# Seven of sixteen state sums moved from VectorE to ScalarE and GpSimd in a two-layer decoder kernel

## What is computed

```python
x = ln(x + mamba(x))            # E=512 channels, N=16 states; stages "pre", "skip", "scan", "out"
x = ln(x + context_softmax(x))  # kv = ctx @ Wk; softmax(norm(x @ kv kv^T))     stage "xat0"
x = ln(x + moe_ffn0(x))         # 8 experts of 176, top 2, shared 352           stage "ffn0"
x = ln(x + hgrn(x))             # gated linear scan over positions              stage "hgrn"
x = ln(x + adjacency(ctx))      # q k^T, top 76 of 256 in each row, sigmoid     stage "adj"
x = ln(x + moe_ffn1(x))         # 8 experts of 128, top 2, shared 256           stage "ffn1"
# mamba: for each state n of 16, over the positions l
state[n] = exp(dts * A[n]) * state[n] + dts * B[n] * hidden
y       += C[n] * state[n]      # then (y + D * hidden) * silu(gate) @ W_out
```

## Time and profile before

| | |
|---|---|
| time, median of 3 runs | 560.07 us (559.85 to 563.25) |
| the profiled execution | 561.63 us, its span 559.8 us |
| granted TensorE clock, mean | 0.938 of full speed |
| PE / PEld busy | 497.2 us (89%) / 435.6 us (78%) |
| DVE / ACT / POOL busy | 472.0 us (84%) / 365.0 us (65%) / 318.8 us (57%) |

### The profile page before, as it was taken

How to read it: one execution, slowest core, us unless ns; L and a number is a source line. 1 busy time by engine, 2 the same in 40 slices (tenths; PEclk the granted TensorE clock), 3 DMA queues, 4 the chain that set the end, 5 groups by cost and what they waited for, 6 DMA issues and landing times.

```text
span 559.8 us, 10385 instructions
## 1 busy us (share of the span) xinstructions
PE 497.2 (89%) x3304; PEld 435.6 (78%) x3304; DVE 472.0 (84%) x1053; ACT 365.0 (65%) x877; POOL 318.8 (57%) x465
## 2 busy tenths in 40 slices
PE   4857376868876999999999999999999999999996
PEld 3535264637765988888898998998999999999985
DVE  1399999979999899999999999999889997745451
ACT  2489967578957866689958797974976481350210
POOL 1056669853688677548946676795649443334042
PEclk9798568679996999999999999999999999999999
DMA  7612920003472454021530566436055206553000
GB/s 192 213 63 74 380 76 2 0 0 104 134 260 90 133 177 134 30 76 58 164 120 5 155 190 220 132 89 194 2 161 170 87 15 211 175 164 105 11 11 9
DMA packets 26517, 64.16 MB, mean 115 GB/s; under 512 B 4512, under 2 KB 8352, under 8 KB 26080
## 3 DMA queue, kind: packets, MB, share of 16 engines
q1 hardware_dynamic: 26464, 63.50, 35.9%
HBM read 62.38 MB, written 1.11 MB: 113 GB/s over the span
## 4 chain that ended last, share of the span: by engine, by line
PE 64%; DVE 16%; issue 8%; POOL 5%; ACT 4%; DMA 2%; SPq 0%; DVEq 0%; POOLq 0%; ACTq 0%
PE work L616 40%; PE work L670 13%; PE h_bank L592 6%; DVE acc L1197 5%; POOL dbu L545 4%; DVE st L1181 3%; PE work L592 2%; DVE m L1144 1%; PE h_bank L693 1%; ACT dA L964 1%; DVE wk L1148 1%; DMA b_rows<-b_dram 1%; DVE du L1113 1%; DVE bst L1016 1%; PE work L749 1%
## 5 line engine op out<-in xcount | busy, mean ns | idle before, releaser
L545 POOL TENSOR_TENSOR dbu<-du,b_rows 128x512 f32<-128x512 f32 x128 | 163.4, 1278 | 30.5 <-DVE du L1133 21.0
L964 ACT ACTIVATE dA<-dts,a_neg 128x127 f32<-128x127 f32 x512 | 156.6, 355 | 21.1 <-DVE st L1181 20.0
L1181 DVE TENSOR_TENSOR_SCAN st<-dA,dbu 128x512 f32<-128x512 f32 x128 | 155.1, 1214 | 3.3 <-ACT dA L964 2.7
L592 PE MATMUL h_bank<-ident,st 128*128 128x128 f32 x512 | 85.8, 302 | 32.8 <-DVE acc L1197 21.8
L616 PE MATMUL work<-xsT,stream 128*128 128x128 f32 x896 | 110.0, 278 | 0.8 <-DVE du L1113 0.7
L616 PEld LDWEIGHTS work<-xsT,stream 128*128 128x128 f32 x896 | 105.9, 194 | 2.8 <-DVE du L1113 0.9
L592 PEld LDWEIGHTS h_bank<-ident,st 128*128 128x128 f32 x512 | 66.3, 156 | 47.9 <-DVE st L1181 38.9
L1197 DVE SCALAR_TENSOR_TENSOR acc<-h_bank,c_cols,acc 128x512 f32<-128x512 f32 x128 | 93.2, 728 | 7.4 <-issue 3.4
L567 POOL TENSOR_TENSOR hb<-hb,wbt 128x512 f32<-128x512 f32 (+2 forms) x48 | 55.2, 1153 | 54.0 <-ACT wbt L836 36.3
L491 POOL TENSOR_SCALAR var<-mv 128x1 f32<-128x1 f32 x56 | 13.1, 234 | 83.5 <-DVE mv L1017 83.1
L670 PE MATMUL work<-stream,hb 128*128 128x256 f32 x224 | 53.6, 381 | 0.0
(11 more groups left out here) (157 smaller groups left out, 795.0 us busy)
## 6 DMA issues: line engine op xcount, KB each, us to landing
stream<-in_stream SPq DMA_DIRECT2D x48, 512.0 KB, 3.8
stream<-in_stream SPq DMA_DIRECT2D x48, 384.0 KB, 3.8
b_rows<-b_dram SPq DMA_DIRECT2D x32, 256.0 KB, 4.5
wg<-in_wg SPq DMA_DIRECT2D x1, 1280.0 KB, 7.7
wu<-in_wu SPq DMA_DIRECT2D x1, 1280.0 KB, 10.3
wd<-in_wd SPq DMA_DIRECT2D x1, 1280.0 KB, 12.9
xT<-in_xT SPq DMA_DIRECT2D x4, 256.0 KB, 4.2
out<-row SPq DMA_DIRECT2D x8, 128.0 KB, 2.1
```

The costliest lines, as they stand in the source:

```text
L545: gp.tensor_tensor(tile, du[:, batch % 2, :, lo:hi], b_rows[:, b % 2, k:k + 1, :].to_broadcast([P, ET, P]), ALU.mult).then_inc(s["dbu_read ...
L592: return nc.tensor.transpose(dst, src, ident[:, :])
L964: last = A(dA[i % DA_RING][:, t, 1:P], dts[:, batch % 2, t, lo + 1:hi], ACT.Exp, scale=a_neg[:, t, k:k + 1])
L1181: V.tensor_tensor_scan(st[:, i % ST_RING].rearrange("p t l -> p (t l)"), dA[i % DA_RING].rearrange("p t l -> p (t l)"), dbu[:, i % DBU_RIN ...
```

## The change

States 1, 3, 5, 7, 9, 11 and 13 of each unit (SHARED) are no longer summed by DVE. ACT multiplies the turned state by its column of C on the way out of PSUM into a new tile, share (one buffer), which frees the bank (semaphore scaled); POOL then adds share to acc (semaphore summed). Both do so one step of the scan later than DVE did, in their own chain step k = n + 3. ACT waits for POOL's sum before it overwrites share; POOL waits for DVE's sum of state n - 1; DVE's sum of state n + 1 waits for POOL's. The other nine states are summed as before.

Of the inputs, the first batch's part of ctxT, the two adjacency weights and gam become a load part of their own (7), issued after part 1 and ahead of 2 to 6. The squares of hgrn (sq) are written into tf, the place of the forget gates; so ACT waits, ahead of a unit's forget gates, for PE's sum of squares of the unit before. All order strings and BANK are new. In the strings, the first round of the adjacency stands behind the first batch's preparation and the second batch's first two steps on DVE, where it stood ahead of them.

```diff
...
+SHARED = (1, 3, 5, 7, 9, 11, 13)
 GROUPS = [(b, lt, 1) for b in range(B) for lt in range(LT)]
...
         "g": [("ffn1", u, k) for u in range(U) for k in F1.steps],
-        "l": [("load", part, 0) for part in range(7)],
+        "l": [("load", part, 0) for part in (0, 1, 7, 2, 3, 4, 5, 6)],
         "b": [("store", b, 0) for b in range(B)],
...
 ORDER = {
...
     "dve": [
-        "ppaaaaappappppsspssaasssssasasasassssssaassssssssssmmmmmssmsssssssmmppppppmpasmsssmssssffmmmmmsffaaassmafffaas",
...
+        "pppppppppaaaaassssssasssassasssssassasassssssasssmmmmmsasmsasmmsmassmssmppppppffpsssffaaassssfssaaasssmmmmmasm",
...
     "pool": [
-        "ssssssssssssssspppppppppppppssssssssmmmsssssssssmmsssspssssssmmmsmmmmmmssssssmmfffffffssssmmmsppppppfffmmfffhs",
...
+        "sssssssssssssssssssssssmmmsssssssmmsssmmmssssmmppppppppppppppssssmmmmssssshsssssmmssfffffffssmmmfffssssssmmfff",
...
     "sp": [
-        "llllllccccbrbrlrcccccccwcxrbccwccrccccrccccccccccccccccccbwoccccocwccccccrrccccccccccccwcoccccccccccccwccocccc",
+        "llllllccblcrbcrlwrcccxcrccccbccccccccccrccwrbccccwccccccccoccccwccccccorccrcccwcccccccccowccccccccccccccccoccc",
...
         loads.append((w_in[:, :, E:2 * E], d["w_in"][:, :, E:2 * E], 4))
-        loads.append((ctxT[:, :, :], d["ctxT"].rearrange("c (b l) -> c b l", b=B), 4))
+        loads.append((ctxT[:, 0, :], d["ctxT"][:, 0:L], 7))
+        loads.append((ctxT[:, 1:B, :], d["ctxT"][:, L:B * L].rearrange("c (b l) -> c b l", b=B - 1), 4))
         for b in range(2, 3):
...
         loads.append((xT[:, 1], d["xT"][:, :, L:2 * L], 4))
-        wqT = load("wqT", [C, C], d["wqT"], 4)
-        wkT = load("wkT", [C, C], d["wkT"], 4)
+        wqT = load("wqT", [C, C], d["wqT"], 7)
+        wkT = load("wkT", [C, C], d["wkT"], 7)
         wkvT = load("wkvT", [C, C], d["wkvT"], 4)
         b_k = load("b_k", [C, 1], d["b_k"], 4)
-        gam = load("gam", [P, 1], d["gam"].partition_broadcast(P), 4)
+        gam = load("gam", [P, 1], d["gam"].partition_broadcast(P), 7)
         w_out = load("w_out", [P, ET, H], d["w_out"], 5)
...
         wd1 = load("wd1", [P, F1.k_tiles, H], d["wd1"], 6)
-        PARTS = 7
+        PARTS = 8
...
         acc = sb("acc", [P, ACC_RING, E])
+        share = sb("share", [P, E])
...
         o = sb("o", [P, 2, HT, P])
-        sq = sb("sq", [P, HT, P])
+        sq = tf
...
         names = """ones_ready consts_ready who_ready a_exp a_ready gam_tanh conv0 hs_ready exp_ready sp_ready dts_ready du_ready
-            dA_ready dbu_ready scan_done h_full skip_read acc_done carry_ready carried dA_cleared keep_exp keep_ready
+            dA_ready dbu_ready scan_done h_full skip_read acc_done scaled summed carry_ready carried dA_cleared keep_exp keep_ready
             th_ready adj_ready mask_ready yg_ready yg_offered q_offered att_max att_exp nmx_ready dsc_ready
...
         turned_at = {key: i for i, key in enumerate(turned)}
-        accs = {key: i + 1 for i, key in enumerate(key for key in turned if key[1] >= 0)}
+        accs = {key: i + 1 for i, key in enumerate(key for key in turned if key[1] >= 0 and key[1] not in SHARED)}
+        sums = {key: i + 1 for i, key in enumerate(key for key in turned if key[1] in SHARED)}
         skips = {key[::2]: i + 1 for i, key in enumerate(key for key in turned if key[1] < 0)}
+        def added(g, n, j):
+            return (s["summed"], sums[g, n, j]) if n in SHARED else (s["acc_done"], accs[g, n, j])
+        def bank_free(g, n, j):
+            return (s["scaled"], sums[g, n, j]) if n in SHARED else (s["acc_done"], accs[g, n, j])
...
                         gp.tensor_tensor(tile[:, :, 0], tile[:, :, 0], carry[:, k, :], ALU.add).then_inc(s["carried"], 1)
+                if stage == "scan" and k - LAG - 1 in SHARED:
+                    n = k - LAG - 1
+                    for j in range(widths[b]):
+                        u = first_unit(b) + j
+                        pool.wait_ge(s["scaled"], sums[b, n, j])
+                        pool.wait_ge(*added(b, n - 1, j))
+                        gp.tensor_tensor(acc[:, u % ACC_RING, :], acc[:, u % ACC_RING, :], share[:, :], ALU.add)\
+                            .then_inc(s["summed"], 1)
                 if stage == "out" and k == 2 and b in OFFERED:
...
                     else:
-                        pe.wait_ge(s["acc_done"], accs[g, n, j])
+                        pe.wait_ge(*bank_free(g, n, j))
                 return h_bank[i % H_BANKS]
...
                 if stage == "adj" and k == 0:
-                    if b == 0:
-                        pe.wait_ge(loaded[4], part_size[4])
+                    if b < 2:
+                        pe.wait_ge(loaded[(7, 4)[b]], part_size[(7, 4)[b]])
                     t = claim("qk", b)
...
                         pe.wait_ge(loaded[4], part_size[4])
+                        pe.wait_ge(loaded[7], part_size[7])
                     if lt == 0:
...
                     if b == 0:
-                        act.wait_ge(loaded[4], part_size[4])
+                        act.wait_ge(loaded[7], part_size[7])
                         A(gth[:, :], gam[:, :], ACT.Tanh, scale=0.5).then_inc(s["gam_tanh"], 1)
...
                         A(acc[:, u % ACC_RING, :], h_bank[at % H_BANKS][:, :], ACT.Copy).then_inc(s["skip_read"], 1)
+                if stage == "scan" and k - LAG - 1 in SHARED:
+                    n, batch = k - LAG - 1, GROUPS[b][0]
+                    if n == SHARED[0]:
+                        act.wait_ge(*read("cT", batch))
+                    for j in range(widths[b]):
+                        u, at, i = first_unit(b) + j, turned_at[b, n, j], sums[b, n, j]
+                        act.wait_ge(s["h_full"], at + 1)
+                        if i > 1:
+                            act.wait_ge(s["summed"], i - 1)
+                        A(share[:, :], h_bank[at % H_BANKS][:, :], ACT.Copy, scale=c_cols[:, batch % 2, u % LT, n:n + 1])\
+                            .then_inc(s["scaled"], 1)
                 if stage == "scan" and k < N:
...
                 if stage == "hgrn" and k == 2:
+                    if b:
+                        act.wait_ge(*full("ss", b - 1))
                     evacuate("hf", b, flat(tf[:, :, :]), work_bank("hf", b)[:, 0:HT * P], func=ACT.Tanh, scale=0.5)
...
                             .then_inc(s["scan_done"], 1)
-                    if k >= LAG:
+                    if k >= LAG and k - LAG not in SHARED:
...
                             else:
-                                dve.wait_ge(s["acc_done"], accs[b, n - 1, j])
+                                dve.wait_ge(*added(b, n - 1, j))
                             V.scalar_tensor_tensor(out=acc[:, u % ACC_RING, :], in0=h_bank[at % H_BANKS][:, :],
```

52 lines of the change are left out of this document (26 added, 26 removed).

## The result

The changed kernel took 569.53 us (median of 3 runs, 569.14 to 569.85) against 560.07: ratio 1.0154, 95% interval 1.0109 to 1.0199. It is 9.5 us slower; 553.0 was forecast, and the range (543 to 567) misses it. The profiled span is 567.7 us (before: 559.8).

The account below looks back on a forecast made before the run. The prediction took the front to 216 us as paced by DVE, then a PE queue without holes. Span 559.8 - 8.3 (front gain) + 1.3 (charge for POOL and DVE) = 552.8 us, so 553; range 543 to 567.

Parts of the forecast that it names:

- More contention: DVE beside POOL: a few of 48 normalizations more turn long, 3 us at most, 0 to 0.7 us of the front.
- Behind it the queue of PE work is the same: After unit 3's end: PE's remaining work is unchanged, so an earlier unit 3 carries through to the end.
- the 8.3 us: Front, to unit 3's end: it comes 8.3 us earlier, at 207.9 us, all of it holes of PE gone.
- about equal work: PE's string at unit 3's end: three more mixer steps and one ffn0 step less than before, taken as equal.
- queue of PE work with no holes: After 216 us: PE is busy 251.8 of 254 us, its four longest waits together 2.0 us.
- 77%: covered: POOL after 216 us: 195.7 of 254 us busy with the added sums, so they fit.
- The front sum: Units 0 to 3: DVE's terms put unit 1's end at 115.3 us and unit 3's at 207.9.
- the charge: Front: 1.3 us added because DVE and POOL, both over 90% full in strict order, do not both keep pace.
- the early rounds: Front, DVE: first four adjacency rounds, formerly free ahead of dts, now cost 5.8 us, less 1.1 for PE's product.
- the third rival: Front: the whole 18 us comes if DVE would have idled at the moved rounds and PE's clock rises; 542 us, chance 0.10.
- POOL becomes the pace: From unit 2 on: POOL's ordered waits stay, unit 3 ends at 221.3 us, late sums delay PE; 569.7 us, chance 0.18.
- Eaten in the front: Front: POOL's and DVE's queues hold each other up, or early rounds cost more; 557 to 562 us, chance 0.32.

Follow-up runs that it names:

- cut: Nearly all of GpSimd's wide work cut short, parts of the result left out: changed kernel 554.08 us, ratio 0.9890; kernel before 556.27 us, ratio 0.9912.
- padded: GpSimd's wide instructions replaced by one power, three one-column products and a short operation: changed kernel 559.73 us, ratio 0.9972; kernel before 557.51 us, 0.9950.
- q_after: Changed kernel with each wide GpSimd instruction replaced by one power, three one-column products and a short operation: 559.73 us, ratio 0.9972.
- e1_strings_only: Changed kernel's strings and early load part, but all sixteen sums on VectorE as before: 588.36 us, ratio 1.0482.
- e3_short_sum: Changed kernel with GpSimd's sum over 16 of its 512 columns only, every wait and ScalarE copy kept: 564.63 us, ratio 1.0041.
- p_after: Changed kernel with each wide GpSimd instruction replaced by two one-column powers and a short operation, slightly longer than the original: 568.65 us, ratio 1.0131.
- rounds: Changed kernel with the first adjacency's rounds put back ahead of dts on VectorE: 575.98 us, ratio 1.0271.

## Why the prediction was wrong

**The whole difference, in ratios.** In the order cut, padded, whole: the changed kernel 0.9890, 0.9972, 1.0154; the one before 0.9912, 0.9950, 1. Of the 1.54%, overlap is 1.82 less 0.50 = 1.3 (7.4 us), hours 0.82 less 0.38 = 0.4 (2.5 us), and the change by itself -0.2 (-1.2 us). Each term is known to 0.6 or 0.7 per cent, so only the overlap is clear of zero.

**The miss, in spans.** The forecast was 552.8 us. With the overlap gone the profiled span is 557.5 (q_after), 4.7 more; with it, 567.7, another 10.2. The first part is the second failed step below (5.8, less 1.1 that the front came earlier), the second part the first.

**The step that failed is "More contention"**: "so a few of the 48 more will be long, 3 us at most, spread over the span and mostly after 216 us: 0 to 0.7 us of the front". Overlap lengthened VectorE's work by 31.2 us in the changed kernel (462.0 against 430.8 padded) and by 6.8 before (472.0 against 465.2), 24 us more. The step had the rule, and had seen a long du and a normalization of 1.381 us in the rows. It multiplied the wrong thing: it scaled the long cases with GpSimd's busy time, a fifth more; but what counts is how often a form of two SBUF operands, a copy or a scale comes beside a wide instruction, and that is set by the order of both engines' work: with the new strings and GpSimd's old load it was already 674 ns (e1_strings_only). It also priced the normalization alone; the router's copy (0.97 us for 0.17), its weights (1.38 for 0.29) and the o scans (2.72 for 0.75, two of them) lose about as much a time. What part of the order does it stays open.

**"Behind it the queue of PE work is the same"** failed too. The forecast gave the stretches behind unit 3 no change; even with the overlap gone they take 349.4 us (q_after) against 343.6. Half of it is work that had been put behind: PE is busy 338.3 us there against 335.2 (248.8 + 86.4), so the 8.3 us were not holes alone, "about equal work" was 3 us off. The kernel before, behind unit 3:

```profile
216.20:467.20 251.00, 248.77 (x1815) 227.00 (x1814) 236.72 (x535) 189.42 (x443) 159.88 (x237) 1.00 0.36 112
467.20:559.80 92.60, 86.41 (x639) 81.54 (x638) 48.23 (x159) 21.85 (x45) 28.28 (x43) 0.99 0.29 90
```

Two of the rows by line and shape between the ends of units 3 and 7 that grew, of the kernel before and then of the changed one (a few others shrank, by less):

```profile
L670 PE MATMUL work<-stream,hb 128*128 128x256 f32 x126 | 30.3, 381 | 0.0
...
L616 PE MATMUL work<-hs,w_x 128*32 128x256 f32 x8 | 1.9, 382 | 0.0
```

```profile
L692 PE MATMUL work<-stream,hb 128*128 128x256 f32 x134 | 32.2, 383 | 0.0
...
L638 PE MATMUL work<-hs,w_x 128*32 128x256 f32 x8 | 1.9, 382 | 0.0
L638 PE MATMUL work<-hs,w_x 128*128 128x256 f32 x7 | 1.7, 379 | 0.0
```

The changed kernel has 4.7 us of PE's busy time more than q_after there (343.0 against 338.3) with 2464 against 2463 matmuls: nearly the same ones, longer. Where it has holes the granted clock is lower, 0.83 between 350 and 360 us, and 1.00 there in q_after. The "queue of PE work with no holes" wasn't a property of the stretch. I take it that it held for as long as VectorE was ahead of PE by more than its next delay; how far ahead it is I hadn't looked, and no run measures it. "77%: covered", said of GpSimd after 216 us, was wrong in the same way: covered for its hours, not for what it does to its neighbour.

**What held.** The front sum: unit 3's end was forecast at 207.9, 209.2 with the charge, and is at 208.1 once the overlap is taken out; unit 1's at 115.3, measured 117.1. But two terms of it were off against each other: the early rounds cost 0.3 us and not 5.8 less 1.1, for VectorE would have stood there for dA, as the third rival supposed; so some 6 us of other cost in units 0 and 1 has no name in my sum. That the front came out right is partly luck. The charge of 1.3 us had no row behind it either. First scan 42.3 (43.6). ACT's copy 676 ns (690; bounds 600 and 780), and ACT's total 397.7 (404). GpSimd's total 387.1 (390), a sum 1279 ns. 72 sums on VectorE. VectorE at 429 to 431 (near 430) with the overlap gone, 462 with it.

**The rivals.** "POOL becomes the pace" has the right time, 569.7, by luck, for it goes another way: unit 3 ends at 211.4 and not at 221.3, and PE waits for VectorE, once for a share, 0.4 us, between 180 and 205 us. Its hours are the smaller term (0.4%). "Eaten in the front" had the wrong place. The advice of the Trainium skill (GPSIMD Engine Reference, section 4.1) to leave elementwise sums to VectorE gave the right sign; what the sums themselves cost is e3_short_sum's 1.1%, known to half a per cent.

## What to carry to other kernels

Before moving work to GpSimd, list every VectorE instruction that has two SBUF operands or is a plain copy or scale, however small, and count up to a whole GpSimd instruction (1.0 to 1.1 us here) for each that may fall beside one; then ask who stands behind it in VectorE's order. A queue that shows no holes is no cushion: look how far ahead its suppliers are. And to tell overlap from hours, pad with one-column instructions and measure the pad from start to start before believing it: 0.09 us too long on 228 of them turned the answer round here, and on the 172 of the kernel before it moved next to nothing.

## What the runs showed of the hardware that wasn't expected

Where the same work started later, TensorE was granted a lower clock, and the same matmuls took 3 us longer. In the changed kernel's strings the stretch from the end of unit 0 to that of unit 1 holds 157 or 158 matmuls; they took 31.0 us of PE at a mean clock of 0.80 in q_after and in the changed kernel, and 34.2 and 34.1 at 0.74 in p_after and in rounds, whose units 1 ended at 123.1 and 121.9 us and not at 117.1. The windows of five us of q_after and then of p_after (columns as above):

```profile
95.00:100.00 5.00, 3.31 (x12) 2.44 (x11) 4.24 (x7) 4.98 (x13) 4.48 (x20) 0.50 0.78 236
100.00:105.00 5.00, 2.65 (x18) 1.70 (x16) 4.87 (x7) 4.96 (x12) 4.30 (x17) 0.99 0.00 0
105.00:110.00 5.00, 4.75 (x22) 3.40 (x23) 4.27 (x8) 4.34 (x14) 4.17 (x18) 1.00 0.00 0
110.00:115.00 5.00, 4.48 (x31) 3.48 (x30) 4.87 (x12) 3.10 (x12) 4.84 (x5) 1.00 0.01 3
```

```profile
95.00:100.00 5.00, 1.72 (x10) 1.08 (x10) 3.73 (x6) 4.97 (x14) 4.62 (x12) 0.76 0.29 84
100.00:105.00 5.00, 4.62 (x18) 3.91 (x19) 4.34 (x8) 4.95 (x10) 4.31 (x12) 0.56 0.46 159
105.00:110.00 5.00, 2.85 (x14) 2.05 (x13) 4.31 (x7) 4.99 (x16) 4.48 (x13) 0.78 0.00 0
110.00:115.00 5.00, 5.00 (x16) 3.75 (x14) 4.29 (x9) 2.03 (x5) 4.62 (x10) 0.54 0.00 0
```

q_after is at the upper level (2.4 GHz) from 100 us on, p_after changes between the two until 115. PE is idle for over a quarter of the time from the end of unit 0 to that of unit 1 in both. p_after and rounds were 3.0 and 1.9 us behind q_after and the changed kernel at the end of unit 0, 6.0 and 4.7 at the end of unit 1, and 9.4 and 6.2 at the end. That the lower clock is what adds the 3 us is argued from these rows and wasn't tried alone.

GpSimd's scaling of one 128x512 tile took 1490 ns, more than its product of two, 1311, and beside it VectorE's two-operand forms had no wait (473 ns; 479 alone), while the copy of two columns had (566; 161 alone). The root on GpSimd, one column, takes 0.57 us on the median, where its other operations of one to four columns take 0.19 to 0.22.
